# A combine-and-prepare stage with a buffer for every result group, the second add on GpSimd and quantising mid-way

## The reference

```
x = x + 0.5 * moe(layernorm(x))            # top 2 of 8 experts per token, results weighed by a gate
x = x + attention(layernorm(x))
x = x + 0.5 * moe(layernorm(x))            # its results are combined in the stage of this change
x = x + 0.5 * fp4_ffn(layernorm(x))        # weights in blockwise fp4, needs them quantised once
x = x + t5_attention(layernorm(x))         # adds position_bias[head, query, key] from a table
x = x + 0.5 * fp4_ffn(layernorm(x))
```

## Time and profile before

| what | us |
|---|---|
| median of 3 runs | 2871.54 |
| the three runs | 2871.42, 2871.54, 2878.43 |
| span of the profiled execution | 2876.9 |
| stage C1, from the first result load to the next stage | 1129.60 to 1213.80 |

### The profile page before, as it was taken

One profiled execution on the slowest core, in us unless ns is written; L12 is line 12 of the kernel. 1 busy time (PEld: TensorE's weight loads), 2 busy tenths in 40 slices (PEclk: granted clock), 3 DMA queues, 4 the chain that ended last, 5 costly groups with the idle time before them and its releaser, 6 DMA issues. The chain is left out here.

```text
span 2876.9 us, 65315 instructions
## 1 busy us (share of the span) xinstructions
PE 2208.8 (77%) x16651; PEld 1787.0 (62%) x16651; DVE 2284.5 (79%) x8269; ACT 1827.3 (64%) x4872; POOL 1399.6 (49%) x1366
## 2 busy tenths in 40 slices
PE   2229994773339993078849999999999999996787
PEld 2229884563339882046627777777777777775565
DVE  5427996875428996779859999999999999997897
ACT  3215552543225552356539999999999999996564
POOL 3765776005756774046504444444444444443554
PEclk9999997895569996589969999999999999998999
DMA  5134442303144444300024333333333333331000
GB/s 166 53 82 124 129 127 88 110 1 118 53 94 126 128 127 123 111 1 0 0 66 95 92 93 93 93 94 94 93 92 92 92 92 92 92 92 45 11 22 26
DMA packets 277442, 238.97 MB, mean 83 GB/s; under 512 B 35732, under 2 KB 262868, under 8 KB 276484
## 3 DMA queue, kind: packets, MB, share of 16 engines
q1 hardware_dynamic: 254644, 196.20, 26.3%
q0 software_dynamic: 17408, 35.82, 4.0%
q10 hardware_dynamic: 5200, 4.84, 0.5%
HBM read 59.31 MB, written 44.24 MB: 36 GB/s over the span
## 5 line engine op out<-in xcount | busy, mean ns | idle before, releaser
L2162 POOL TENSOR_TENSOR p_prob<-p_prob,p_inverse 128x512 f32<-128x512 f32 x512 | 533.2, 1042 | 662.8 <-DVE p_inverse L1990 662.8
L2081 ACT ACTIVATE p_prob<-p_neg,p_neg_max 128x256 f32<-128x256 f32 x1024 | 511.8, 509 | 9.9 <-DVE p_neg_max L1984 8.6
L1994 DVE SCALAR_TENSOR_TENSOR p_probT<-p_t_ps,p_probT 128x512 f16<-128x512 f32 x512 | 352.7, 689 | 65.5 <-ACT p_probT L2087 49.0
L1984 DVE CUSTOM_DVE_ANT_0 p_neg<-p_s_ps,top_bias 128x256 f32<-128x256 f32 x1024 | 390.9, 420 | 11.7 <-PE p_s_ps L2234 11.4
L709 POOL DMA_INDIRECT rows_by_expert<-p_r_z,p_r_target x256 | 248.3, 970 | 299.7 <-DVE p_r_z L564 181.5
L1022 POOL DMA_INDIRECT results_by_token<-p_e_result,p_e_slot x288 | 284.5, 988 | 158.3 <-DVE p_e_result L965 81.8
L2087 ACT ACTIVATE p_probT<-p_t_ps 128x512 f16<-128x512 f32 x512 | 306.4, 598 | 19.2 <-issue 16.1
L2243 PE MATMUL p_t_ps<-top_ident,p_prob 128*128 128x128 f32 x2048 | 310.4, 274 | 1.1 <-POOL p_prob L2162 1.0
L859 PE MATMUL p_e_o_ps<-p_w,p_e_hT 128*128 x2304 | 281.5, 275 | 0.4 <-issue 0.2
L2188 PE MATMUL p_o_ps<-p_probT,p_val 128*128 128x256 f16 x1024 | 279.2, 273 | 1.5 <-DVE p_probT L1994 0.5
L2190 PE MATMUL p_o_ps<-p_probT,p_val 128*128 128x256 f16 x1024 | 279.1, 273 | 0.0
(11 more groups left out here) (280 smaller groups left out, 5830.0 us busy)
## 6 DMA issues: line engine op xcount, KB each, us to landing
p_k_stack<-p_qkT SPq DMA_DIRECT2D x512, 128.0 KB, 2.3
p_q_stack<-p_qkT SPq DMA_DIRECT2D x512, 64.0 KB
p_e_z<-rows_by_expert SPq DMA_DIRECT2D x144, 129.0 KB
p_e_affine<-p_affine SPq DMA_DIRECT2D x144, 128.0 KB, 2.0
p_got<-results_by_token SPq DMA_DIRECT2D x64, 256.0 KB, 2.9
p_e_b<-p_b SPq DMA_DIRECT2D x144, 64.0 KB
results_by_token<-p_e_result,p_e_slot POOLq DMA_INDIRECT x288
p_r_w<-in_w SPq DMA_DIRECT2D x2, 2048.0 KB, 8.3
```

Of the source, the lines that this page charges most:

```text
L1984: ins = v.tensor_tensor_reduce(neg[k % 2][:, t, :], s_ps[k % 2][:, t, :], bias[:, t, h, :], -1.0 / SCORE_SCALE, HUGE, ALU.add, ALU.min, ne ...
L1994: v.scalar_tensor_tensor(probT[k % 2][:, 1, :, :], t_ps[k % 2][:], PROB_SCALE, probT[k % 2][:, 0, :, :], ALU.mult, ALU.subtract).then_inc( ...
L2081: ins = act.activation(prob[k % PROBS][:, t, :], neg[k % 2][:, t, :], ACT.Exp, bias=neg_max[k % 2][:, t:t + 1], scale=-1.0, accum_out=tota ...
L2162: pool.tensor_tensor(prob[k % PROBS][:], prob[k % PROBS][:], inverse[k % PROBS][:].unsqueeze(2).to_broadcast([P, SEQ_TILES, SEQ]), ALU.mult)\
```

## The change

`got` gets room for all 16 groups, so that SP's wait for a free buffer goes. On ACT the write of the bias and its two reads are pulled apart: ACT weighs groups 0 and 1 between them, then groups 2 to 9, then turns the bias round and copies the weights, then weighs groups 10 to 15. The second add is moved from DVE to POOL, which runs all sixteen. DVE takes the statistics of a group two groups behind its first-choice adds, and quantises the weights after group 5 instead of after group 7. The stage A0 keeps the old order of adds on DVE.

```diff
--- before.py
+++ after.py
@@ -1087,7 +1087,7 @@
             ins = act.activation(got, got, ACT.Copy, scale=self.gate[:, 1, t])
         ins.then_inc(self.weighted, 1)
 
-    def add(self, v, i, first=0):
+    def add_first(self, v, i, first=0):
         for r in range(GT):
             if r % self.HALF == 0:
                 v.wait_ge(self.landed[r // self.HALF], i * 16 + 16)
@@ -1096,12 +1096,18 @@
             got = self.of_tile(i, first, r, 0)
             ins = v.scalar_tensor_tensor(x, got, self.gate[:, 0, t], x, ALU.mult, ALU.add)
         ins.then_inc(self.added_one, 1)
-        v.wait_ge(self.weighted, i + 1)
-        v.sem_inc(self.carried, 1)
-        v.wait_ge(self.added_one, i + 1)
+
+    def add_second(self, eng, i, first=0):
+        eng.wait_ge(self.weighted, i + 1)
+        eng.sem_inc(self.carried, 1)
+        eng.wait_ge(self.added_one, i + 1)
         xg = self.x_res[:, bass.ds(i * GT, GT), :]
         second = self.got[:, bass.ds((i - first) * (GT * TOP_K), GT * TOP_K), :].rearrange("p (t k) d -> p t k d", k=TOP_K)[:, :, 1, :]
-        v.tensor_tensor(xg, xg, second, ALU.add).then_inc(self.added, 1)
+        eng.tensor_tensor(xg, xg, second, ALU.add).then_inc(self.added, 1)
+
+    def add(self, v, i, first=0):
+        self.add_first(v, i, first)
+        self.add_second(v, i, first)
         v.wait_ge(self.added, i + 1)
         v.sem_inc(self.carried, 1)
 
@@ -1699,9 +1705,11 @@
         sp.dma_start(self.table[:], self.a["bias_table"]).then_inc(self.loaded, 16)
         sp.dma_start(self.bucket_of[:], self.a["bucket_of"]).then_inc(self.loaded, 16)
 
+    def write(self, act):
+        act.wait_ge(self.kept, 1)
+        act.dma_start(self.vec_dram, self.vec[:]).then_inc(self.written, 16)
+
     def skew(self, sp):
-        sp.wait_ge(self.kept, 1)
-        sp.dma_start(self.vec_dram, self.vec[:]).then_inc(self.written, 16)
         sp.wait_ge(self.written, 16)
         for t in range(SEQ_TILES):
 
@@ -1721,6 +1729,11 @@
         for t in range(SEQ_TILES):
             act.activation(self.bias[:, t, :, :], self.reversed[:, t, :, ::-1], ACT.Copy, scale=SCORE_SCALE).then_inc(self.bias_ready, 1)
         act.wait_ge(self.bias_ready, SEQ_TILES)
+
+
+C1_STATS_LAG = 2
+C1_QUANTISE_AT = 6
+C1_TURN_AT = 10
 
 
 def combine_and_prepare(nc, name, x_res, ident, bias, w_up_gate, w_down, norms, combine, a):
@@ -1731,7 +1744,7 @@
         position = PositionBias(nc, m, bias, a)
         link = m.sem("link")
         if combine:
-            combine.allocate(m, GROUPS // 2)
+            combine.allocate(m, GROUPS)
         block = stack.enter_context(nc.Block())
 
         @block.sync
@@ -1749,35 +1762,51 @@
             position.load(act)
             weights.load(act)
             position.keep(act)
-            position.skew(act)
-
-            def weigh_groups(first, last, base):
-                loop_groups(act, first, last, lambda i: combine.weigh_second(act, i, base))
+            position.write(act)
+
+            def weigh_groups(first, last):
+                loop_groups(act, first, last, lambda i: combine.weigh_second(act, i))
 
             if combine:
                 combine.weigh_second(act, 0)
-                weigh_groups(1, GROUPS // 2, 0)
+                combine.weigh_second(act, 1)
+            position.skew(act)
+            if combine:
+                weigh_groups(2, C1_TURN_AT)
             position.turn_round(act)
             weights.keep(act)
             if combine:
-                weigh_groups(GROUPS // 2, GROUPS, GROUPS // 2)
+                weigh_groups(C1_TURN_AT, GROUPS)
+
+        @block.gpsimd
+        def _(pool):
+            if combine:
+                combine.add_second(pool, 0)
+                loop_groups(pool, 1, GROUPS, lambda i: combine.add_second(pool, i))
 
         @block.vector
         def _(v):
             chain = Chain(v, link)
 
-            def complete(i, first=0):
-                combine.add(v, i, first)
+            def statistics(i):
+                v.wait_ge(combine.added, i + 1)
                 norms.raw(v, i * GT, GT, x_res)
+
+            def complete(i):
+                combine.add_first(v, i)
+                statistics(i - C1_STATS_LAG)
 
             weights.zero(v)
             chain.restart()
             if combine:
-                complete(0)
-                loop_groups(v, 1, GROUPS // 2, complete)
+                for i in range(C1_STATS_LAG):
+                    combine.add_first(v, i)
+                loop_groups(v, C1_STATS_LAG, C1_QUANTISE_AT, complete)
             weights.quantise(v, chain)
             if combine:
-                loop_groups(v, GROUPS // 2, GROUPS, lambda i: complete(i, GROUPS // 2))
+                loop_groups(v, C1_QUANTISE_AT, GROUPS, complete)
+                for i in range(GROUPS - C1_STATS_LAG, GROUPS):
+                    statistics(i)
 
 
 def bias_attention(nc, name, x_res, ident, bias, norms, a):
```

## The result

The changed kernel takes 2864.99 us (median of 6 runs, 2860.99 to 2866.73) against 2874.95 for the kernel before in 6 runs taken in turn with them (2871.42 to 2878.43): a ratio of 0.9967 with a 95% interval of 0.9956 to 0.9977, 10 us or 0.33% faster. The prediction said 10.3 us less. Its time of 2861.2 is 3.8 us too low, since it started from the median of three runs of before, 2871.54, and that of all six is 3.4 higher; 2864.99 lies in its full range (2857 to 2868.5), but above that of its case 1 (2857 to 2863).

The account below looks back on a forecast made before the run. Stage C1 was taken as paced by result loads until about 1163, then mostly by DVE's work and its waits for ACT. Group 15's start 1197.2 + 4.3 + 0.5 = 1202.0 against 1212.28: 10.3 us less, 2861.2, range 2857 to 2868.5.

Parts of the forecast that it names:

- case 1: Stage C1 bound by DVE, POOL mostly beside the statistics, or by loads: gain 8.6 to 13 us, chance 0.66.
- The sum: Stage C1 ends at 1202.0 instead of 1212.28, 10.3 us earlier, and everything behind it moves with it.
- the late weighing: ACT releases the adds of groups 10 and 11, which may stretch DVE's first-choice adds; 0.5 us taken.
- the prediction's last sentence: Forecast fails if four adds take 2.4 in most groups, statistics wait for POOL, or last load moves over 2 us.
- Quantising mid-way: In C1, quantising after group 5 starts 9.4 us of DVE work 7.9 us earlier; called the main gain.
- The second add on GpSimd: C1's second add on POOL takes 1.18 us, excludes DVE's two-input adds, and makes a cycle of 2.6 us.
- The lower bound of 2.3: DVE's cycle per group in C1 if POOL's add never holds it: 2.3 us instead of 3.32.
- What would show it: Signs in the changed profile, among them a 2.6 us cycle and four first-choice adds at 1.2 to 1.5 us.
- rival 2: GpSimd and DVE collide in most groups of C1, four adds stretched to 2.46: gain 1.4 to 8.6 us, chance 0.24.
- the price of GpSimd's add: If POOL's add cost over 3.5 us, C1's cycle would be 4.8 and the kernel slower, 2882 us; chance 0.04.
- the loads did not come later: Against the claim that bias reads slow C1's load stream and eat the whole gain: 2871.5 us, chance 0.06.
- the 5.4 us: How much longer the profiled execution, 2876.9 us, was taken to be than the median of the runs, 2871.5.

## Why the prediction was right, point by point

- **The sum.** Forecast 10.3 us less, measured 10. Stage C1 gave 11.6, 1.3 more than forecast. Quantising ended 44.1 us after the first load, as forecast, and group 15 started 22.6 us later, where 23.4 + 0.5 had been taken: the cycle of group 6 was only 1.84 us, as its four adds met no add of GpSimd, and the late weighing cost 0.3. The loads behind group 5 had no part in it, as DVE came later than they did. Their last landed 63.9 us after the first instead of 66.0, 2.1 us earlier, which by the prediction's last sentence would be a sign of failure; the other kernels with two loads under way have 62.9 to 65.7, with the bias reads first or not, so it is hardly more than the scatter of single executions. Of the 11.6 some 1.5 seem to be given back in bias attention: 1196.4 to 1197.6 us in the changed kernel and the four nearest to it, 1195.5 and 1195.7 in the two that have DVE's code of before. ACT's idle time put down to issue goes with it, 16.5 to 17.2 us in those five and 16.1 and 16.3 in these two; that this too is the place of the code is argued, not shown. That 10 meets 10.3 so closely is luck to that extent: 1.3 more in the stage, 1.5 less behind it.
- **Quantising mid-way.** "That is the main gain" was wrong, though its times were right to 0.1 us. Put back after group 7 it costs 0.4 us, an estimated 0.9 with the same landings. The step that failed: I counted the 7.9 us by which quantising starts earlier, and not the two groups that DVE then still has to do. The gain is DVE's time per group (3.32 to 2.57 us; of the sixteen groups, the ten behind quantising count), and the wait of 4.5 us for group 8's weighing. The forecast's end rests on that cycle as well, so its sum is right where its sentence on the main gain is not.
- **The second add on GpSimd.** The duration (1.18 forecast, 1.26 measured), the exclusion and the cycle of 2.6 were right. The lower bound of 2.3 was not: the loop itself makes 2.5. And the cycle is right by two misses that cancel, which is luck. POOL's add ends 1.64 us after the release, not about 1.4, since in the loop POOL starts 0.37 us after it and not 0.1 (without the loop it is 0.08). But from there DVE needs only 0.93 us, not 1.18, since the held add ends 0.15 after POOL's. So 1.64 + 0.93 stands where the forecast had 1.4 + 1.18. The four adds take 0.68 us longer, not 0.3, as DVE asks for them 0.7 us after the release and not 1.1: with 1.86 us they lie outside the 1.2 to 1.5 of "What would show it", and short of the 2.4 of its failure. The ratio of 1.96 from the Trainium skill ("GPSIMD Engine Reference", section "Performance versus the Vector engine") gave an estimate of 1.36 us for the add; the trace has 1.26 to 1.27, and decides.
- **ACT.** The bias reads were not 0.7 us later but as late as before. Late weighing of group 10 cost one stretched group of four adds (2.13 us) and a cycle of 2.84: 0.3 us, 0.5 was taken.
- **The rivals.** A part of a collision came in every group, but not the 2.46 us of rival 2, because GpSimd's add is released by the very instruction after which DVE turns to its statistics; the price of GpSimd's add was far from 3.5 us; the loads did not come later. Two readings were off without touching the sum. The loads were in 13.5 us ahead of group 15's adds (1209.14 less 1195.6), and 17 ahead only of the last statistics. And the 5.4 us set a span beside times from outside, which in the runs with both numbers are 1.8 to 2.2 us longer than the span.

## What to carry to other kernels

Moving an operation to GpSimd beside DVE pays if it is released where DVE turns to one-input work: here a 1.26 us add cost DVE 0.07 us a group, in a loop that idled 0.35 us at that place anyway; with the loop written out POOL's round still sets the cycle, at 2.28 us, and what the add costs there is not measured. Judge an early start by what the engine has still to do after it, not by how much earlier it starts: 5.8 us later cost 0.4 to 0.9. And after any edit compare the stages that it did not touch: with other code ahead of it a long loop took up to 28 us more in 1200, and 63 idle memsets gave 15 back.

## What the runs showed of the hardware

- The 128x512 f32 add on GpSimd with two SBUF inputs took 1.26 us (1.27 beside DVE), and DVE's four adds of 128x128 took 1.86 us beside it and 1.18 without. The held one of the four ended 0.15 us after GpSimd's add.
- Two loads of 256 KB under way moved a group of 512 KB in 3.35 us; four under way, with the stage written out, had all 32 loads issued in 44 us instead of 61, eight in 42.
- 63 memsets of one column on DVE took 1.18 us together, 19 ns each.
- A stage of which no instruction was changed took 1194.5 to 1225.0 us, with 59 to 188 packets of instruction fetches in the whole program. The packets alone do not tell the time (124 with 1209.6 us, 122 with 1197), but they count the engines with idle time put down to issue in that stage: 59 with none, 121 to 124 with one, 186 and 188 with two.
